# Unread TensorE products at five places of the ramp of a two-layer kernel

## The reference, cut to what matters

```python
x = L0_attn_hidden_states                       # 4 sequences x 1024 tokens x 128
x = _layernorm(x + _L0_attn_ref(x, ...))        # gated delta rule in chunks of 32 tokens, 4 heads
x = _layernorm(x + _L0_ffn_ref(x, ...))         # 8 experts: router, softmax of the top two, GELU
x = _layernorm(x + _L1_attn_ref(x, ...))        # linear recurrence over time (LRU) with two gates
x = _layernorm(x + _L1_ffn_ref(x, ...))         # gated input layer, two hidden 512x512 layers, output
return x
```

## Time and profile before

| | us |
|---|---|
| median of the 3 runs | 802.26 |
| the runs | 802.26, 1057.01, 798.42 |
| the profiled execution | 804.78 |
| its span, first to last instruction | 803.0 |
| PE busy | 759.0 (95%) |
| DVE busy | 576.1 (72%) |
| ACT busy | 498.2 (62%) |
| POOL busy | 491.5 (61%) |
| mean granted clock of PE | 0.974 |

### The profile page before, as it was taken

How to read it: one execution, slowest core, us unless ns; L and a number is a source line. 1 busy time by engine, 2 the same in 40 slices (tenths; PEclk the granted TensorE clock), 3 DMA queues, 4 the chain that set the end, 5 groups by cost and what they waited for, 6 DMA issues and landing times.

```text
span 803.0 us, 11422 instructions
## 1 busy us (share of the span) xinstructions
PE 759.0 (95%) x3525; PEld 581.9 (72%) x3525; DVE 576.1 (72%) x1150; ACT 498.2 (62%) x799; POOL 491.5 (61%) x504
## 2 busy tenths in 40 slices
PE   8999999989979799999989999999999999999996
PEld 5777786777667567766777778767867787777775
DVE  5786788697669677687777777777777677776553
ACT  6877645335945565567557755774577467677753
POOL 0069699279988565987586347544754474386343
PEclk9999899789999899999999999999999999999998
DMA  4135526323131400141014002301230120021000
GB/s 144 54 106 146 168 70 180 108 80 96 37 115 51 112 14 27 53 105 28 27 53 133 27 27 63 95 26 29 63 94 24 40 65 13 1 82 39 0 14 13
DMA packets 47820, 52.68 MB, mean 66 GB/s; under 512 B 2784, under 2 KB 32224, under 8 KB 47776
## 3 DMA queue, kind: packets, MB, share of 16 engines
q1 hardware_dynamic: 47776, 52.13, 22.4%
HBM read 38.62 MB, written 13.50 MB: 65 GB/s over the span
## 4 chain that ended last, share of the span: by engine, by line
PE 67%; DVE 11%; POOL 8%; issue 6%; ACT 5%; DMA 2%; SPq 0%; DVEq 0%; ACTq 0%; POOLq 0%
PE bank L466 67%; POOL fbl L1370 3%; POOL acc L1378 2%; DVE spread L1631 1%; POOL tmp L1311 1%; POOL tpm L1314 1%; DVE sexp L1639 1%; DVE m L1688 1%; DVE x L1622 1%; DVE fbl L1838 1%; POOL texp L1338 1%; DVE yg L1649 1%; DMA conv<-in_conv 1%; DVE x3h L1855 1%; POOL fbl L1413 1%
## 5 line engine op out<-in xcount | busy, mean ns | idle before, releaser
L1370 POOL TENSOR_TENSOR fbl<-hf,fbh 128x512 fp32r<-128x512 f32 x64 | 90.2, 1409 | 40.8 <-ACT fbh L1161 40.4
L1149 ACT ACTIVATE hf<-bank 128x512 f32<-128x512 f32 x64 | 38.2, 598 | 123.0 <-PE bank L466 101.1
L1311 POOL TENSOR_TENSOR tmp<-apm,tpm 128x31 f32<-128x31 f32 (+15 forms) x124 | 73.5, 593 | 42.5 <-DVE apm L1503 34.4
L1838 DVE TENSOR_TENSOR fbl<-hf,fbh 128x512 fp32r<-128x512 f32 x64 | 69.2, 1082 | 39.4 <-ACT fbh L1155 37.1
L1314 POOL TENSOR_TENSOR tpm<-tpm,tmp 128x31 f32<-128x31 f32 (+15 forms) x124 | 77.1, 622 | 9.7
L1378 POOL TENSOR_TENSOR acc<-acc,yg 128x512 f32<-128x512 f32 x48 | 69.8, 1454 | 21.1 <-DVE yg L1649 21.1
L1413 POOL TENSOR_TENSOR fbl<-hf,fbh 128x512 fp32r<-128x512 f32 x28 | 37.0, 1324 | 72.6 <-DVE fbh L1905 72.6
L466 PE MATMUL bank<-fal,wfh 128*128 128x512 f32 x160 | 67.8, 423 | 0.0
L466 PE MATMUL bank<-fbl,wmh 128*128 128x512 f32 x128 | 60.0, 469 | 8.0 <-POOL fbl L1370 5.0
L466 PE MATMUL bank<-fah,wfh 128*128 128x512 f32 x160 | 62.5, 390 | 0.0
L466 PE MATMUL bank<-fah,wfl 128*128 128x512 f32 x160 | 62.2, 389 | 0.0
(11 more groups left out here) (246 smaller groups left out, 2155.6 us busy)
## 6 DMA issues: line engine op xcount, KB each, us to landing
gb<-gt SPq DMA_DIRECT2D x64, 256.0 KB, 3.2
pk<-pack SPq DMA_DIRECT2D x7, 1280.0 KB, 7.1
pack<-pk SPq DMA_DIRECT2D x5, 1280.0 KB, 6.9
ws<-in_wf SPq DMA_DIRECT2D x11, 256.0 KB, 2.8
pack<-pk SPq DMA_DIRECT2D x4, 640.0 KB, 4.0
xs<-in_xh SPq DMA_DIRECT2D x8, 262.0 KB, 2.8
xt<-in_xh SPq DMA_DIRECT2D x8, 262.0 KB, 2.9
ws<-in_wm SPq DMA_DIRECT2D x8, 256.0 KB, 3.3
```

The costliest lines, as they stand in the source:

```text
L1149: A.activation(hf[:, 0, :], bank[4][:, :], ACT.Gelu).then_inc(S["gelu_done"], 1)
L1311: G.tensor_tensor(m, a, r, ALU.mult).then_inc(S["t_mul"], 1)
L1370: G.tensor_tensor(fbl[:, sl, :], hf[:, 1, :], f32(fbh[:, sh, :]), ALU.subtract)\
L1838: tt(fbl[:, sl, :], hf[:, 0, :], f32(fbh[:, sh, :]), ALU.subtract).then_inc(S["lo0"], 1)
```

## The change

Unread products are added at five places on PE, 42 in all; nothing is removed or moved, and the other engines' programs are as before. The first group multiplies tap weights into bank 0 because it stands ahead of the first use of the expert weights; the others use `keep_busy`.

```diff
@@ the lead, tile 4
                 else:
                     project(t + 1, 0)
+                    for _ in range(5):
+                        mm(bank[0][:, :], wtaph[:, 0, 0, :], wtaph[:, 0, :, :])
                 gram(t, 0)
                 gram(t, 1)
@@ ramp2(a, s)
                 attention_heads(a)
                 gram(s, 0)
                 attention_var(a)
-                keep_busy(6, 0)
+                keep_busy(9, 0)
                 router(a)
+                keep_busy(3, 0)
                 pe.wait_ge(S["ws_lo"], WM // PIECE)
                 pe.wait_ge(S["rs_ln"], 2 * (s + 1))
                 up(a, 0)
@@ dense(m, a, f, inv)
                         if first and m == 1 and e == 0:
                             pe.wait_ge(*after("lg_ready", a))
+                        if first and (m, e) in ((0, 3), (1, 1)):
+                            keep_busy(10, 7)
                         (delta_state if e % 2 else delta_in)(a, e // 2)
@@ dense, at its end
                 if first and m == 1:
+                    keep_busy(11, 7)
                     pe.wait_ge(*after("rs3", 1))
```

## The result

| kernel | runs | median us | lowest to highest |
|---|---|---|---|
| before | 19 | 800.38 | 796.74 to 807.05, and one of 1057.01 |
| changed | 19 | 796.86 | 795.14 to 799.14 |

The ratio is 0.9949 with a 95% interval of 0.993 to 0.9968. That is 3.5 us less in the medians and 4.0 in the means (800.9 and 796.9), where 9.5 had been forecast. The profiled execution of the changed kernel took 799.14 us, the slowest of its 19, with a span of 797.3 us against 803.0: 5.7 us less.

The account below looks back on a forecast made before the run. PE was taken as the bound, at half clock behind short waits, with DVE next in places. Savings of 3.0 + 4.4 + 0.1 + 0 + 2.0 = 9.5 us from 802.26 gave 793 us, range 788 to 799.5.

Parts of the forecast that it names:

- Place 1: End of the lead, ahead of the first Gram group: 5 products fill PE's 1.14 us wait, saving 3.0 us.
- Place 2: Round the router: 3 + 3 products in PE waits of 0.84 and 0.55 us, saving 4.4 us.
- Place 3: Ahead of the second delta state, experts of tile 0: 10 products in 3.03 us, saving 0.1, at most 1.5.
- Place 4: Ahead of the first delta state, experts of tile 1: 10 products in 4.04 us, saving 0, at most 1.5.
- Place 5: Ahead of the first gated product: 11 products in a 3.3 us wait, saving 2.0 us.
- The sum: All five places together: 9.5 us saved from the median of 802.26, giving 793 us.
- The range: Forecast interval for the changed kernel's time, 788 to 799.5 us, leaving out some 0.2 of the chance.
- The gate's phase: Rival: once work shifts earlier, clock falls vanish or appear elsewhere; 5.0 us saved, 797 us; chance 0.25.
- The small products are the cause: Rival: clock falls behind places 1 and 2 despite fills; only place 5 pays, 2.0 us, 800; chance 0.08.
- The overrun at the low level: Rival: fills at places 2 to 5 run at 0.41 us a product, delaying 3.5 us, 806; slower chance 0.03.

Follow-up runs that it names:

- p34: Kernel before plus ten unread products each at places 3 and 4 alone; mean 801.1 us against 801.8 beside it, ratio 0.9982.
- dve_short: Changed kernel with one DVE transpose in the experts of tile 0 cut from 32 to 4 blocks; mean 794.1 us against the changed kernel's 796.3.
- p125: Changed kernel without the products at places 3 and 4; mean 796.5 us against the changed kernel's 796.3, ratio 0.9943 to the kernel before.
- p12: Kernel before plus the fills at places 1 and 2 alone; mean 798.6 us, ratio 0.9970 to the kernel before.
- before_b: Kernel before, unchanged, profiled again; that execution took 804.62 us at a clock of 0.974.
- before_a: Kernel before, unchanged, profiled once more; that execution took 799.73 us at a clock of 0.983.
- p1: Kernel before plus the five products at place 1 alone; mean 800.0 us, ratio 0.9995 to the kernel before.
- long34: Changed kernel with twenty products instead of ten at places 3 and 4; mean 795.1 us against the changed kernel's 796.3.

## Why the prediction was right or wrong

- **Place 1, 3.0 us.** Right where the clock falls without the fill: 3.16. DVE took back 0.85 of it, which was not in the sum.
- **Place 2, 4.4 us.** Right where the clock falls without the fill: 4.5. The second fill of three holds the first expert product by 0.1 us (139.95 behind the router at 138.25, before 142.17 behind 140.56), at the low end of the 0.1 to 0.2 foreseen. The gate copy came at 146.04, where about 145.5 had been named.
- **Place 3, 0.1 us.** Right in the end, and for the reason given: DVE sets the pace (p34, dve_short). One thing that would have shown it did not come: the delta-in product was to come as much earlier as place 2 had given "and no more", and came 1.3 us earlier than that, near the bound of 1.5. What was missed is that this gain becomes a new wait for DVE there, and that the clock could fall behind it.
- **Place 4, 0 us.** Not told from 0 in the mean (p125 and p34; some 0.7 us in the profile of p34), and the mechanism was open as the prediction had it: the wait left was 1.72 us (it was 4.04), and the clock held through such a wait in two profiles and fell in four. In the profiled execution of the changed kernel it held, and the gain was lost behind 237.92.
- **Place 5, 2.0 us.** Right: 2.2 in the profile, 2.0 in the mean (p12 to p125). The fall behind it stands in all three profiles of the kernel before.
- **The sum** is the step that failed. It took 9.5 us, read off one execution, from the median of all. That execution was at 804.78 with a clock of 0.974, and the prediction treated its 2.5 us over the median as noise. They came with the falls at places 1 and 2. These are in some executions and not in others: before_b has them, before_a has not. Their fills are worth 3.2 us (2.3 behind the next waits for DVE) and 4.5 us where the clock would fall, and nothing where it holds: 1.0 and 1.4 in the mean, where the sum had 3.0 and 4.4. In the mean the steps are 1.0 + 1.4 + 0.2 for places 3 and 4 + 2.0 = 4.6 us; that they come to the 4.0 to 4.6 measured (796.9 and 796.3 against 800.9) is no second proof, as they are steps of one ladder of kernels. The range held since it was wide enough for this rival: that the time lies inside it is owed to the range, not to the sum. That three of the four profiles without the fills show the falls, and only 3 in 10 of the timed runs, may be chance with so few.
- **The rivals.** The gate's phase came out, with 797. It was put forward for falls that move when the program shifts; that happened (168, 240, 401 us), but the larger part was that the falls to be cured were not always there. The prediction cited the Trainium skill (TensorE: Matmul & The Clock Gate, part 1) for one kernel showing differing numbers of slow products from run to run. The page says so of the products at a kernel's start; before_a and before_b, at 0.983 and 0.974, show it in the middle of one. The Trainium skill's rule that the prediction cited against places 1 and 2 (same page, "Why this matters for your kernels"), that only much longer gaps cost the clock, does not hold here: with gaps of 1.14 and 0.84 us the clock fell in two of three profiles of the kernel before, and filling them gave 2.4 us in the mean. "The small products are the cause" falls, since they ran at 1.00 in every profile with the gaps filled. The overrun at the low level did not occur: the fills' products took 0.24 us each.
- **Open.** What decides, from one execution to the next, whether the clock falls at a place is not shown by any run.

## What to carry to other kernels

A low stretch of the clock in one profile is not a property of the kernel: profile it several times, or read the mean clock of the timed runs, and multiply what a cure saves by the share of runs that need it. Ask of each low stretch who waits for PE behind it: where DVE set the pace, 11 us less of low clock came to 0.7 us in a pair of profiles that are alike otherwise, and 1.8 us less work on DVE were worth about 2; where PE was busy all the time, 6.8 us of low clock cost 3.1. A fill can move the wait on to the next point where the other engine is late, so look there for the next fall before counting the gain.

## What the runs showed that was not expected

- The time follows the mean clock closely from run to run: over 33 runs of the kernel before (beside p1, without the one at 0.932), each us of low clock goes with 0.33 us of time, and over all 86 with 0.34. Over the variants with place 1 filled it is 0.23 to 0.29, and 0.35 over p34. A straight line through those 33 meets zero low clock at 791 us, through those of the changed kernel at 793.4. That the second is higher is not explained; it may be the line, since the low stretches that were cured are the costly ones.
- An unread product at the full level costs 0.23 to 0.24 us, and fills that held a delta step up by 2.9 us cost nothing in the profile of long34, where DVE was later still.
- The same subtraction on DVE of 128 x 512 takes 0.67 us to 1.78 us in the experts of tile 0. In the profiled execution of the changed kernel this, and not only the clock, stretched DVE's way through the stage. Which of the two came first, and what lengthens the subtraction, was not tried.
